# Attention on one Trainium2 core: mask products that write 64 output rows each

## The reference

```python
qkv = x @ Wqkv                                    # 16 heads of 8
logits = jnp.einsum('bihd,bjhd->bhij', q, k) * scale
logits = logits + SLOPES[None, :, None, None] * rel[None, None, :, :]
causal = pos[:, None] >= pos[None, :]
logits = jnp.where(causal[None, None, :, :], logits, -jnp.inf)
attn = jax.nn.softmax(logits, axis=-1)
out = jnp.einsum('bhij,bjhd->bihd', attn, v).reshape(Bc, Tc, Dc)
return out @ Wout
```

## Time and profile before

| | |
|---|---|
| three runs | 901.35, 901.40, 901.77 us; median 901.4 |
| profiled execution | span of 899.3 us from first to last instruction (its own total is not listed apart) |
| mean granted TensorE clock | 0.876 |
| busy TensorE, weight loads | 633.2 us (70%), 468.5 us (52%) |
| busy VectorE, ScalarE, GpSimd | 635.0 (71%), 445.1 (49%), 456.7 us (51%) |
| attention stage, mask products | first at 403.5 us, last near 660 us |
| L1875, masks of `maxima` | 512 products |
| L1868, masks of `scores` | 512 products |

### The profile page before, as it was taken

The page is one execution under the profiler, slowest core; times in us unless marked ns, Lnnn a source line. Parts: engine busy times, 40 slices in busy tenths (PEclk is TensorE's granted clock), DMA queues, the critical chain, the costliest instruction groups (busy, mean ns, idle before and its releaser), DMA issues. The chain is left out here.

```text
span 899.3 us, 21979 instructions
## 1 busy us (share of the span) xinstructions
PE 633.2 (70%) x7826; PEld 468.5 (52%) x7826; DVE 635.0 (71%) x1395; ACT 445.1 (49%) x873; POOL 456.7 (51%) x569
## 2 busy tenths in 40 slices
PE   0197973882059999324799998998963795999950
PEld 0073432562049999312566665665641564998850
DVE  6989988681048888387677777877741972888855
ACT  5632167670035555271766665665642242555534
POOL 1126767887637777510002222554573881677760
PEclk9978997896579999755899999999985997999985
DMA  9510001432134563242121322332111412454418
GB/s 287 132 37 1 0 0 45 83 80 58 44 60 90 102 93 84 85 162 60 45 83 50 91 73 73 78 105 74 49 36 37 80 34 48 84 97 93 93 27 281
DMA packets 131850, 70.51 MB, mean 78 GB/s; under 512 B 89535, under 2 KB 118725, under 8 KB 131746
## 3 DMA queue, kind: packets, MB, share of 16 engines
q1 hardware_dynamic: 121042, 50.46, 23.8%
q0 software_dynamic: 9088, 16.88, 6.9%
q10 hardware_dynamic: 1616, 1.77, 0.7%
HBM read 26.61 MB, written 30.50 MB: 64 GB/s over the span
## 5 line engine op out<-in xcount | busy, mean ns | idle before, releaser
L1437 ACT ACTIVATE ARENA<-banks,ARENA 128x256 f32<-128x256 f32 x312 | 122.2, 474 | 104.2 <-PE banks L1400 86.7
L2150 DVE TENSOR_REDUCE ARENA<-banks 128x4 f32<-128x1024 f32 (+1 forms) x128 | 122.7, 959 | 46.7 <-PE banks L1891 45.4
L1398 PE MATMUL banks<-ARENA,W1H 128*128 128x256 f16 x312 | 87.1, 279 | 65.3 <-DMA ARENA<-slots 58.2
L2072 ACT ACTIVATE ARENA<-banks 128x1536 f32<-128x1536 f32 x64 | 92.8, 1450 | 58.2 <-PE banks L1919 58.2
L1412 PE MATMUL banks<-W2L,ARENA 128*128 x624 | 110.8, 220 | 3.2 <-DVE ARENA L1450 2.4
L1414 PE MATMUL banks<-W2H,ARENA 128*128 x624 | 110.2, 219 | 0.0
L1413 PE MATMUL banks<-W2H,ARENA 128*128 x624 | 110.1, 219 | 0.0
L1388 POOL DMA_INDIRECT expert_out_g<-ARENA x78 | 80.6, 1034 | 47.7 <-issue 25.8
L1388 POOL DMA_INDIRECT expert_out_f<-ARENA x78 | 80.0, 1026 | 37.5 <-issue 25.8
L1471 DVE TENSOR_TENSOR ARENA<-ARENA 128x1024 f16<-128x1024 f32 x78 | 95.6, 1226 | 2.7
L1000 POOL DMA_INDIRECT slots<-ARENA,PLACE x64 | 77.6, 1212 | 28.4 <-issue 20.4
(11 more groups left out here) (312 smaller groups left out, 1812.0 us busy)
## 6 DMA issues: line engine op xcount, KB each, us to landing
spread<-ARENA SPq DMA_DIRECT2D x96, 64.0 KB, 2.1
ARENA<-expert_out_f SPq DMA_DIRECT2D x8, 512.0 KB, 7.4
ARENA<-spread SPq DMA_DIRECT2D x16, 256.0 KB, 3.0
ARENA<-spread SPq DMA_DIRECT2D x32, 128.0 KB, 3.0
ARENA<-expert_out_g SPq DMA_DIRECT2D x8, 512.0 KB, 7.3
XT<-in_w SPq DMA_DIRECT2D x10, 256.0 KB, 7.7
slots<-EMPTY SPq DMA_DIRECT2D x16, 129.0 KB, 4.5
ARENA<-in_w SPq DMA_DIRECT2D x8, 256.0 KB, 6.8
```

What stands on the lines that cost most here:

```text
L1398: pe.matmul(out, t.W1H[:, e, ms], XST[i][:, 0], start=True, stop=False)
L1437: ins = nc.scalar.activation(HF[i % 2][:, m], UP[i % 2][:, m], ACT.Gelu, bias=BIAS[i % 4][:, m:m + 1], scale=1.0 / WS)
L2072: nc.scalar.activation(PR[x % 2], t.psum_all[:, 5:8, :], ACT.Exp, scale=1.0 / LOGIT).then_inc(exps, 1)
L2150: dve.tensor_reduce(MX[:, G // 2, tile, :, :, G % 2].rearrange("p s a -> p a s"), src, AX.X, ALU.max).then_inc(m_red, 1)
```

## The change

Each mask product now has 64 output rows (`PAIR[half]`) in place of 128. A group still has four: two bands of operand rows by two halves of output rows, of 256 columns (the half in which all 128 columns of a block matter) and of 128 columns (where only 64 do). Each starts its own half of the bank, and the identity is always the same 64 x 64 one. In `maxima` the order is by halves, then bands. In `scores` the second mask of `late[1]` stands ahead of `early_scores(0)`; before, it stood behind it. No wait is added or removed, and no other engine's instructions change.

```diff
--- before.py
+++ after.py
@@ -1861,18 +1861,21 @@
                         ins = pe.matmul(ps[0][:, js], x[:, c, js], w[:, 0:D], start=(i == 0), stop=(i == 2))
                 ins.then_inc(v_mm, 1)
 
-            def mask_later(out, a, part, start):
-
-                first, n = ((HALF + HALF * a, HALF), (HALF * a, P))[part]
-                rows = SPREAD[PAIR[a], first:first + P]
-                pe.matmul(out, rows, LATER[PAIR[a], :, first:first + n], start=start, stop=False, skip_group_check=True)
-
-            def mask_earlier(out, a, part, start):
-
-                first, n = ((HALF + HALF * a, P), (HALF * a, HALF))[part]
-                rows = SPREAD[PAIR[a], first:first + P]
+            def mask_later(out, a, half):
+
+                n = HALF + HALF * half
+                rows = SPREAD[PAIR[a], HALF + HALF * a:P + HALF * a]
+                first = HALF * a + HALF - HALF * half
+                pe.matmul(out[PAIR[half], :, 0:n], rows, LATER[PAIR[a], :, first:first + n], start=True, stop=False,
+                          skip_group_check=True)
+
+            def mask_earlier(out, a, half):
+
+                n = P - HALF * half
+                rows = SPREAD[PAIR[a], HALF + HALF * a:P + HALF * a]
                 first = HALF + HALF * a
-                pe.matmul(out, rows, EARLIER[PAIR[a], :, first:first + n], start=start, stop=False, skip_group_check=True)
+                pe.matmul(out[PAIR[half], :, P - n:P], rows, EARLIER[PAIR[a], :, first:first + n], start=True, stop=False,
+                          skip_group_check=True)
 
             def maxima(y, tile):
 
@@ -1882,10 +1885,9 @@
                 after(pe, m_red, 2 * y + 1 - tile)
                 keys, queries = P * tile + P, slice(P * tile, P * tile + P)
                 out = [ps[2 + a][:, 0:2 * keys].rearrange("p (s n) -> p s n", n=keys) for a in range(2)]
-                for a in range(2):
-                    mask_earlier(out[a][:, :, P * tile:P * tile + P], a, 0, True)
-                for a in range(2):
-                    mask_earlier(out[a][:, :, P * tile + HALF:P * tile + P], a, 1, False)
+                for half in range(2):
+                    for a in range(2):
+                        mask_earlier(out[a][:, :, P * tile:P * tile + P], a, half)
                 for s in range(2):
                     for a in range(2):
                         ins = pe.matmul(out[a][:, s], QPAD[c % 3][PAIR[a], s, G, queries], KST[c % 3][PAIR[a], G, 0:keys],
@@ -1918,18 +1920,18 @@
                 def late_scores(a):
                     return pe.matmul(ps[7][:, SEQ * a:SEQ * a + SEQ], KST[c % 3][PAIR[a], G, P:2 * P],
                                      QPAD[c % 3][PAIR[a], :, G, P:2 * P], start=False, stop=True, skip_group_check=True)
-                mask_later(late[0], 0, 1, True)
-                mask_later(early[1], 1, 1, True)
-                mask_later(late[0][:, :, 0:HALF], 0, 0, False)
-                mask_later(early[1][:, :, 0:HALF], 1, 0, False)
+                mask_later(late[0], 0, 1)
+                mask_later(early[1], 1, 1)
+                mask_later(late[0], 0, 0)
+                mask_later(early[1], 1, 0)
                 late_scores(0).then_inc(st_mm, 1)
                 early_scores(1)
-                mask_later(early[0], 0, 1, True)
-                mask_later(early[0][:, :, 0:HALF], 0, 0, False)
+                mask_later(early[0], 0, 1)
+                mask_later(early[0], 0, 0)
                 pe.wait_ge(st_mm, 3 * x + 1)
-                mask_later(late[1], 1, 1, True)
+                mask_later(late[1], 1, 1)
+                mask_later(late[1], 1, 0)
                 early_scores(0).then_inc(st_mm, 1)
-                mask_later(late[1][:, :, 0:HALF], 1, 0, False)
                 late_scores(1).then_inc(st_mm, 1)
 
             def weigh(x):
```

## The result

The changed kernel takes 918.95 us (median of 4 runs, 917.71 to 919.30) against 901.38 for the kernel before (4 runs): a ratio of 1.0188, 95% interval 1.0171 to 1.0205, 17.6 us slower. Forecast were 915.5 us and slower; the range of 908 to 928 holds the time. The profiled execution has a span of 917.1 us, 17.8 more than the earlier trace rows.

The account below looks back on a forecast made before the run. TensorE was taken to bound the attention stage, with a hidden wait for VectorE. 64 quarters times 0.285 is 18.2 us, less 4.1 swallowed by waits: 901.4 + 14.1 = 915.5 us, range 908 to 928.

Parts of the forecast that it names:

- the price of a border: s: TensorE's extra time when neighbouring products change between 64*128 and 64*64, taken as 0.095 us.
- The width changes for free: Rival: changing output rows alone costs nothing on TensorE, quarters get 0.105 us shorter, 896 us; chance 0.09.
- The halves don't overlap: Rival: both halves of a band wait for each other, m stays 0.18, quarter costs 0.505 more, 929.5 us; chance 0.06.
- Nothing moves: Rival: array keeps its 64*128 shape, or switch price near 0.053 cancels the savings, 901.4 us; chance 0.05.
- m + s: TensorE time for a group of four masks, m = 0.125 us, plus the change of shape behind it, s = 0.095.
- maxima 0: TensorE's masks and score products for maxima of tile 0: 0.425 us in place of 0.29, +0.135 a quarter.
- maxima 1: TensorE's masks and score products for maxima of tile 1: 0.535 us in place of 0.49, +0.045 a quarter.
- the quarter: One period of TensorE's attention work, 3.64 us on average, forecast 0.285 us longer, 64 of them.
- the wait ahead of maxima 1: TensorE's hidden wait for VectorE's tile 0 maximum, some 0.25 us a quarter, forecast to be used up.
- Other waits: Ten TensorE waits for VectorE between 448 and 641 us, to swallow up to 0.24 each, 2.4 us.
- The first five and last four intervals: Attention's ends: the prediction had first and last four quarters swallow about 0.2 us each, 1.7 us.
- theory B: Explanation weighed by the experiments: the time is lost to a lower TensorE clock or in other stages, not the quarters.

Follow-up runs that it names:

- zero_narrow: Kernel before plus one 64-column product of zeros with 64 output rows in maxima of tile 1, making two borders: 919.09 us, ratio 1.0188.
- all_narrow: Changed kernel with score products also cut into halves of 64 output rows, no border inside maxima or scores: 902.33 us, ratio 1.0008 to the kernel before.
- moved_only: Kernel before with only the second mask of late[1] moved ahead of early_scores(0), masks still wide: 901.72 us, ratio 0.9999.
- zero_wide: Kernel before plus one 64-column product of zeros with 128 output rows in maxima of tile 1, no border: 906.88 us, ratio 1.0045.
- narrow_spread: Changed kernel with score products halved too, and row-maxima spread transfers ahead of the stores on the SP queue: 901.93 us, ratio 1.0000 to the kernel before.
- spread_first: Kernel before with only the SP queue reordered, row-maxima spread transfers ahead of the stores: 901.52 us, ratio 0.9998.
- maxima_narrow: Kernel before with masks and products of maxima all 64*64, scores wide, and spread transfers ahead of the stores: 900.78 us, ratio 0.9992.
- maxima_only: Kernel before with narrow masks in maxima alone, scores masks still 128 rows: 907.53 us, ratio 1.0060.
- scores_only: Kernel before with narrow masks in scores alone, maxima masks still 128 rows: 907.06 us, ratio 1.0052.
- first_wide: Changed kernel with the first group of masks in scores back to 128 output rows: 912.67 us, ratio 1.0109 to the kernel before.
- old_place: Changed kernel with the last narrow mask of late[1] back behind early_scores(0): 941.30 us, ratio 1.0435 to the kernel before.

## Why the prediction was right

The step that decided was the price of a border that differs in output rows only, which no row of before showed. It was taken as 0.095 from changes of other kinds; the trace and zero_narrow give 0.09 to 0.12 (in zero_narrow 0.09 ahead of the added product, and an estimate of 0.12 behind it, the 0.15 less a quarter of the 0.11 that 256 columns take). "The width changes for free" would have needed less than 0.053, and is refuted by zero_narrow. "The halves don't overlap" is refuted by the rows of after, where four masks last no longer than one, and by all_narrow. "Nothing moves" is refuted by the shape in the rows and by the time.

The size was forecast a little low, 14.1 us against 17.6. By terms:
- A group of four masks with its border behind it takes 0.23 to 0.24, against m + s = 0.22. Of it came 0.025 in maxima 0, 0.025 in scores and 0.015 in maxima 1; the quarter of the earlier trace rows grew by 0.35 in place of 0.285. How the 0.23 divides between m and s the rows don't show.
- Quarters differ. The four of a batch grew by 0.29, 0.34, 0.26 and 0.35, in the mean 0.31. In the third the wait ahead of maxima 1 was longer (528.61 to 529.01 before, 0.40, against 0.31 here) and covered more. The prediction took one kind of quarter for all.
- Other waits swallowed 3.5 us, against 2.4: from the exponential of quarter 5 to that of quarter 59 (starts 452.19 and 648.70 before, 454.61 and 664.33 after) the time grew by 13.2, where 54 times 0.31 is 16.7. The prediction counted waits for VectorE alone; 1.3 of the 3.5 is one wait for a transfer, which the changed kernel no longer has. In the trace of before:

```profile
504.08 0.34 PE L1868 MATMUL banks<-ARENA 64*128 64x256 bf16 x4 [1.30 <-DMA ARENA<-ARENA]
```

- The rest of the kernel shifted as a whole, by 0.6 us more than nothing: 17.8 - 13.2 - 2.6 - 1.4, the last two those of the next point.
- The first five and last four intervals were to swallow 1.7. They did not: they grew by 2.6 and 1.4 us (exponentials at 430.34, 452.19, 648.70, 660.89 before; 430.21, 454.61, 664.33, 677.91 after), against 2.8 for nine times 0.31. This is where the forecast fell short. In the 54 intervals between, it makes 54 times 0.285 less 2.4, or 13.0, against 13.2, which is partly luck: a quarter and what the waits swallow were both taken too small. In the first five TensorE had a lower clock than before. The windows view from 428 to 442 us, of the kernel before and then of the changed one:

```profile
428.00:442.00 14.00, 10.56 (x120) 6.93 (x121) 9.30 (x27) 10.26 (x22) 1.83 (x3) 0.77 0.22 69
```

```profile
428.00:442.00 14.00, 12.22 (x98) 5.30 (x96) 8.53 (x25) 8.65 (x17) 1.83 (x3) 0.50 0.22 69
```

The granted clock from 428 to 442 us (the column behind POOL's busy time) is 0.50 in place of 0.77, that is 1.2 GHz throughout. Over the same stretch the six other traces without a border, or with borders only ahead of the wait, have 0.74 to 0.80 (moved_only, zero_wide, all_narrow, narrow_spread, spread_first, maxima_narrow), maxima_only has 0.82, and scores_only, zero_narrow, first_wide and old_place have 0.62 or 0.63. So most kernels with borders have the lower clock here, but maxima_only has not, each is one execution, and the cause stays open. What it may have cost is an estimate of 1.1 us, the 2.6 less five times 0.31. From 448 to 660 us the clock is 1.00 in both kernels, and behind the last exponential the changed kernel takes 0.8 us more (239.2 against 238.4), so theory B is no more than a small part.

That the wait of 0.25 us would be used up, and TensorE itself be late, is what the rows show (no wait ahead of 525.52), and maxima_only with scores_only bring it out best: either half could still hide in it. ScalarE's exponential is no longer than before (1450 ns before, 1451 after, in the median), as forecast.

## What to carry to other kernels

On TensorE, count the changes of shape between neighbouring products before cutting a product to fewer output rows: each cost about 0.1 us here, as long as a product of 256 columns takes to stream (0.11), and the 0.055 us that the overlap could gain is lost at the first of them. Where all neighbours had the same shape, or the border lay ahead of a wait for another engine, narrow products made the steady quarters here 0.06 us shorter, though no kernel as a whole came out faster. Before adding up the price of two edits, look whether both hide in the same wait: it can be spent only once.

## What the runs showed of the hardware beyond that

- Two changes of shape around a product of 64 columns cost 0.22 us; the product itself, in the shape of its neighbours, 0.02 (zero_wide against before, by the batch).
- Four products of 64\*64 run beside each other: a group with two of 256 and two of 128 columns shows 0.30 us from first start to last end, and a single one of 256 has 0.29 by itself.
- A product may start ahead of one that stands before it in the program. In scores_only a score product of maxima 1 (L1893) starts at 521.72 and the last mask (L1877) at 521.77, though all four masks stand before it. So the written order of "The kernel before" is not always the order of starts within TensorE. The rows don't name the bands, but they fit bands that go on one by one: the first mask starts at 521.55, 0.12 after `early_scores(0)` and `late_scores(1)` at 521.43, when the 256 columns of the late product are through (0.11) and the 512 of the early one, on the other band, are not (0.22).
